# GpSimd's eight row gathers in two halves, the second after TensorE's picks of the step before

## The reference

```python
xn = _layernorm(x, axis=-1)
x = x + _L0_gnn_ref(xn, edge_index, ...) + _L0_mix_ref(xn[None], ...)[0]
x = x + _L0_ffn_ref(_layernorm(x, axis=-1)[None], ...)[0]
```

```python
h = (x @ W).reshape(N, H, C)
e = jax.nn.leaky_relu(a_src[src] + a_dst[dst], negative_slope=NEG_SLOPE)
m = jax.ops.segment_max(e, dst, num_segments=N)
p = jnp.exp(e - m[dst])
denom = jax.ops.segment_sum(p, dst, num_segments=N)
out = jax.ops.segment_sum(alpha[:, :, None] * h[src], dst, num_segments=N)
```

## Time and profile before

| what | value |
|---|---|
| median of the three runs | 2849.89 us |
| span of the profiled execution, first to last instruction | 2837.7 us |
| what lies around the span, against the median | 2849.89 - 2837.7 = 12.2 us |
| mean granted TensorE clock in the profile | 0.830 |
| TensorE busy | 71% |
| VectorE busy | 57% |
| GpSimd busy | 51% |
| ScalarE busy | 38% |

### The profile page before, as it was taken

One profiled execution on the slowest core, in us unless ns is written; L12 is line 12 of the kernel. 1 busy time (PEld: TensorE's weight loads), 2 busy tenths in 40 slices (PEclk: granted clock), 3 DMA queues, 4 the chain that ended last, 5 costly groups with the idle time before them and its releaser, 6 DMA issues. The chain is left out here.

```text
span 2837.7 us, 37360 instructions
## 1 busy us (share of the span) xinstructions
PE 2019.8 (71%) x9074; PEld 1433.7 (51%) x9075; DVE 1609.9 (57%) x3942; ACT 1081.1 (38%) x1932; POOL 1458.7 (51%) x1586
## 2 busy tenths in 40 slices
PE   8478887666666666666677777878777856788663
PEld 6355565445555544544445545555545544564331
DVE  7556666446575755865546656666544655553033
ACT  5222222224444533444344455555434443433110
POOL 3455555665666666553445555555553544430156
PEclk9789997777777776778889889889987978899886
DMA  9644444754555555454545544455554544431365
GB/s 311 140 114 132 127 120 111 252 148 137 151 152 145 154 147 140 126 142 136 156 137 139 148 139 135 133 140 141 142 152 116 142 117 109 124 86 56 101 186 174
DMA packets 286906, 401.52 MB, mean 141 GB/s; under 512 B 108835, under 2 KB 209475, under 8 KB 283182
## 3 DMA queue, kind: packets, MB, share of 16 engines
q0 software_dynamic: 74208, 206.08, 27.3%
q1 hardware_dynamic: 194316, 168.88, 20.1%
q10 hardware_dynamic: 18162, 24.08, 2.9%
HBM read 345.72 MB, written 81.83 MB: 151 GB/s over the span
## 5 line engine op out<-in xcount | busy, mean ns | idle before, releaser
L1519 POOL DMA_INDIRECT rows_g<-node_table,src_all x1347 | 1286.4, 955 | 1093.2 <-PE psB L2304 500.2
L2304 PE MATMUL psB<-rows_g,pick_e 128*128 128x260 f32 x2704 | 808.0, 463 | 148.8 <-issue 114.2
L2304 PEld LDWEIGHTS psB<-rows_g,pick_e 128*128 128x128 f32 x2704 | 622.7, 236 | 298.4 <-issue 177.5
L2104 ACT ACTIVATE pick_n<-local_row 128x1024 bf16<-128x1024 bf16 x169 | 178.6, 1057 | 634.2 <-remote 451.9
L1694 DVE TENSOR_TENSOR rows_g<-rows_g,psD 128x2048 f32<-128x2048 f32 x169 | 384.9, 2277 | 0.0
L2381 PE MATMUL psD<-W_f,hidT 128*128 x896 | 274.7, 460 | 0.0
L2345 PE MATMUL psC<-W_f,xnT 128*128 x448 | 231.3, 640 | 0.0
L2293 PE MATMUL psA<-window,pick_n 128*128 128x24 bf16 x1352 | 60.2, 175 | 224.0 <-issue 78.7
L2381 PEld LDWEIGHTS psD<-W_f,hidT 128*128 128x128 f32 x896 | 192.4, 226 | 45.3 <-issue 5.9
L1665 DVE TENSOR_TENSOR pick_e<-psD,slot_all 128x1024 f32<-128x1024 f32 x169 | 203.7, 1205 | 0.0
L1541 POOL DMA_INDIRECT rows_g<-set_dram,places x98 | 96.1, 980 | 206.9 <-issue 181.6
(11 more groups left out here) (381 smaller groups left out, 2966.5 us busy)
## 6 DMA issues: line engine op xcount, KB each, us to landing
local_row<-local_dram SPq DMA_DIRECT2D x169, 256.0 KB
rows_g<-node_table,src_all POOLq DMA_INDIRECT x1347
xin<-sent_dram SPq DMA_DIRECT2D x112, 128.0 KB
set_dram<-xn SPq DMA_DIRECT2D x112, 128.0 KB
xnT<-in_xT_dram SPq DMA_DIRECT2D x96, 128.0 KB
sent_dram<-sorted_dram SPq DMA_DIRECT2D x96, 128.0 KB
sent_dram<-sorted_dram ACTq DMA_DIRECT2D x96, 128.0 KB
acc<-node_table SPq DMA_DIRECT2D x49, 128.0 KB
```

Source lines behind the costliest of these rows:

```text
L1519: pool.indirect_dma_start(out=rows_g[:, r, j], out_offset=None, in_=node_table, in_offset=bass.IndirectOffsetOnAxis(ap=src_all[:, g, j:j + ...
L2104: act.activation(pick_n[:], local_row[:, r], ACT.Relu, bias=1.0, scale=-1.0).then_inc(pick_n_ready, 1)
L2304: last = pe.matmul(ps_sum[s % 2][:, 0:AW], pick_e[:, s % SLOTS, j], rows_g[:, s % RING, j, 0:AW], start=(j == 0), stop=(j == EG - 1))
```

## The change

Inside the loop over a step's eight gathers, ahead of the fifth one (j = EG // 2 = 4), GpSimd now waits until `picked` has reached s, which is when the picks of step s-1 are done, and adds one to its gate. This is so in every step but the first.

```diff
                         pool.wait_ge(summed, s - RING + 1)
                     pool.sem_inc(pool_gate, 1)
                     for j in range(LAST_COLS if s == 0 else EG):
+                        if j == EG // 2 and s >= 1:
+                            pool.wait_ge(picked, s)
+                            pool.sem_inc(pool_gate, 1)
                         pool.indirect_dma_start(out=rows_g[:, r, j], out_offset=None, in_=node_table,
                                                 in_offset=bass.IndirectOffsetOnAxis(ap=src_all[:, g, j:j + 1], axis=0)
                                                 ).then_inc(gathered[r], 16)
```

## The result

The changed kernel takes 2757.45 us (median of 4 runs, 2743.37 to 2765.3) against 2848.8 us for the kernel before: a ratio of 0.965, with a 95% interval of 0.963 to 0.968. That is 91 us less, where 4 us less was forecast, and it lies far outside the range of 2836 to 2858. The prediction was wrong.

A forecast was written before the change was run, and what follows sets the result against it. The prediction took TensorE as the fullest engine (71%), with GpSimd not full, and asked whether its gathers come late. Its terms 0 + 0 + 0 - 4 = -4 us gave 2845.8 us, range 2836 to 2858.

The forecast's parts named there:

- (3): Steps 91 to 168: 64 of 78 steps wait, 232 us in sum, but rows keep 7.9 us of cover; cost nothing.
- the sum's second and third zero: The 0 us terms for steps 3 to 90 and for steps 91 to 168 in the forecast's sum.
- (1): Every step where the wait is already met: the two added instructions on GpSimd cost nothing.
- (2): Steps 3 to 90: 26 of 88 steps wait, 48 us in sum; tight steps 30 to 40 lose nothing.
- (4): The start: fewer backlogged gathers let factors and windows through sooner; second pick gains 0 to 8.6 us, taken as 4.
- Rival A: Slower: the second four gathers land on TensorE's sums, 11 more gaps, +15 us, 2861 us; chance 0.17.
- Rival B: Faster: gathers collide less with SyncE's hand-outs of 24 sorted tiles, -12 us, 2834 us with the start; chance 0.16.
- Rival C: Nothing: the start's gain is 0 to 1 us or is given back, 2849 us; chance 0.17.

The follow-up runs named there:

- c_after: The changed kernel run once more with the same code, against the kernel before: ratio 0.966, 2722.7 us beside 2815.2.
- e1: The change's two instructions, but waiting for sums of three steps before, already met, so gathers keep their times; 2812.3 us beside 2813.9 for the kernel before.
- e3: The change with its wait for the picks only in steps 1 to 84; 2778.1 us beside 2813.9 for the kernel before.
- e5: No wait for picks; the fifth gather waits until the first four have landed; 2760.6 us beside 2815.2 for the kernel before.
- e9: No wait for picks; GpSimd clears a scratch tile once between fourth and fifth gather, a short pause; 0.960 of the kernel before.
- e13: No wait for picks; short pauses of one clearing behind the second, fourth and sixth gather; 2666.8 us beside 2841.7 for the kernel before, 0.939.
- e18: Three clearings in every step, but behind the eighth gather, so the row stays unbroken; 2843.8 us beside 2849.5 for the kernel before.
- e6: The change with its wait ahead of the third gather, so six gathers run behind the picks; 0.992 of the kernel before.
- e4: The change with its wait ahead of the first gather, so all eight run behind the picks; 1.016 of the kernel before.
- e15: No wait for picks; one short pause of one clearing behind the sixth gather, against the kernel before: worth 0.7%.
- e16: The kernel with one short pause between fourth and fifth gather and no wait for picks, in a second set; 0.972 of the kernel before.
- e10: No wait for picks; six larger clearings between fourth and fifth gather, a gap of 4.24 us against 0.30; total time not given.
- e17: Short pauses behind the second, fourth and sixth gather, and behind every gather in steps 85 to 168; 0.970 of the kernel before.

## Why the prediction was wrong, point by point

**The step that failed is (3)**, "Cost: nothing", with the sum's second and third zero. It followed the gathers to their reader, found 7.9 us of cover, and stopped there. The cover was right: in the changed kernel L1686 waits for gathers once by name, 5.1 us, and some 9.6 us at the start (113.92 above). What it left out is that a row of gathers acts on others than its reader: TensorE's signals to ScalarE and GpSimd come late while it runs. The moved wait was priced at nothing in both directions, and its gain is nearly all of the 91 us: in steps 84 to 142 alone 52 us, by c_after against e1.

**Steps (1) and (2).** (1) holds, shown by e1. (2) counted waits in 26 of 88 early steps, 48 us in sum, and took the effect for nothing; e3, with the wait in steps 1 to 84, earns 36 us.

**Step (4), the start.** The mechanism held and was undersized at its place: 8.6 us at the second pick for the 4 forecast. But nothing of it is left at the readers of steps 1 and 2, since the rows of step 1 landed later than its working had them, 9.0 us behind their last gather. From the turn-taking that the Trainium skill states (DMA: Bandwidth & Descriptors, section on queues, rings and completion order) the prediction had an estimate of 3 us; the measured 8.6 us is larger, though it is the other operand, pick_n, that ends the wait now, and no run here tests the rule by itself.

**Rival A** had its sign, and more than its price of 15 us: 16 more gaps, 30 us more. It was outweighed. **Rival B** had the right side and the right half of the kernel ("a shorter stretch from 1260 us on") but another cause. Its price of 12 us was a tenth of a collision between gathers and hand-outs in each of 24 tiles; what the runs show is a collision of gather rows with TensorE's signals. "In the late steps the gathers move by 3.6 us in the mean, and their number stays" was the argument against it, and just this delay is the break. **Rival C**, that nothing would come of it, was wrong.

What the trace of before would have shown: of 441 signals of TensorE that are seen over 1 us late, 426 end within a row of gathers or up to 2 us behind it, while ScalarE's and VectorE's come in time.

**What is shown, and what not.** Shown: the gain comes with a break within the row of gathers (e5, e9, e13), not with the instructions (e1), not with GpSimd's extra work (e18), not with a place behind the picks (e6, e4 against e5 and e9). Shown in the traces: signals of TensorE that fall into the later part of a row are late, others hardly ever, and the other engines' are not. That these late signals are what the change's gain comes from is the best account, not a measured sum: the runs with the longest or the most breaks have the smallest mean delay (over all of TensorE's matched signals 1.3 us in e5 and 1.1 in e13, against 2.4 in e1), and the runs without a gain have that of e1 (2.5 in e18, 2.3 in e15). But the change has 2.0 us and e16 2.3, and the share of signals over 1 us late hardly tells them from the kernels without a break: 43 and 46%, against 47 in before and 42 in e1.

Open: by which path. The times point at the traffic more than at the issuing: in e1 a row's first packets start 1.6 us behind its first gather and its last ones 1.8 us behind the end of the last gather (both medians), and the held signals come some 1.7 us behind it. No run separates the two. A gather that moves fewer bytes would; it wasn't tried.

## What to carry to other kernels

A GpSimd queue that isn't full and whose results come in time can still cost time: look at what other engines exchange while its gathers run. Try to break long rows of indirect DMAs with pauses of about a microsecond: three pauses in a row of eight were worth 6% here, nearly twice as much as the change. Time each choice, since rows that come too late for their reader cost more than further or longer pauses give (e10, e17), though some late rows are borne (e13). And where a wait seems to cost nothing, price it in both directions before it gets a zero.

## What was not expected of the hardware

A semaphore that TensorE raises during an unbroken row of indirect DMAs is seen 4.2 us late in the median (93 turns of e1), usually some 1.7 us behind the end of the row's last gather, against 0.01 us outside of a row (46 turns). The first 3 us of a row hold nearly nothing (2 of 202 signals of e1), and semaphores of ScalarE and VectorE aren't held at all (0.01 us in the mean, 976 of them). A pause of 1.01 us from gather to gather, 0.7 us more than normal, lets a third of the held signals through (24 of 73 in e16) and is worth 3 to 4% behind the fourth gather, 0.7% behind the sixth of eight. One of 2.66 us lets them all through (257 of 257 in e5). A clearing of 128 columns on GpSimd takes 0.22 us, but a wait for it and the next gather behind it add 0.79 us.
